# Queries of a cross attention made for two tiles at once, from high and low halves

## The reference

```python
Q = (x @ Wq.T).reshape(B, xN, NUM_HEADS, HEAD_DIM)
KV = (z @ Wkv.T).reshape(B, zN, 2, NUM_HEADS, HEAD_DIM)
K, V = KV[:, :, 0], KV[:, :, 1]
attn = softmax(einsum('bqhd,bkhd->bhqk', Q, K) * SCALE)
O = einsum('bhqk,bkhd->bqhd', attn, V).reshape(B, xN, DIM)
return O @ Wo.T
```

## Time and profile before

| | |
|---|---|
| runs | 1501.46, 1505.46, 1506.04 us; median 1505.46 |
| the profiled execution | 1500.6 us, its span 1498.8 us |
| busy over the span | TensorE matmul 1436.7 us (96%), weight load 1284.1 (86%), VectorE 1087.7 (73%), ScalarE 807.3 (54%), GpSimd 544.1 (36%) |
| DMA | 174.10 MB, 116 GB/s over the span |
| setup block | 3.7 to 19 us |
| cross attention | 19 to 687 us, its first scores at 32.35 us |
| tile 1, tile 13, tile 14, tile 15 begin at | 72.16, 557.03, 597.43, 637.40 us |

### The profile page before, as it was taken

One profiled execution on the slowest core, in us unless ns is written; L12 is line 12 of the kernel. 1 busy time (PEld: TensorE's weight loads), 2 busy tenths in 40 slices (PEclk: granted clock), 3 DMA queues, 4 the chain that ended last, 5 costly groups with the idle time before them and its releaser, 6 DMA issues. The chain is left out here.

```text
span 1498.8 us, 39481 instructions
## 1 busy us (share of the span) xinstructions
PE 1436.7 (96%) x14944; PEld 1284.1 (86%) x14944; DVE 1087.7 (73%) x1941; ACT 807.3 (54%) x1525; POOL 544.1 (36%) x814
## 2 busy tenths in 40 slices
PE   7999999999999999998899998799999999999998
PEld 6888888888888888876788787688999999999997
DVE  3677777777677776775567686797887878787885
ACT  4666666666666666654333434345555555555452
POOL 1222222222222222234866877453332333334232
PEclk9999999999999999999999999799999999999999
DMA  6301101100001100100001104179877878787871
GB/s 238 126 26 30 30 22 28 28 23 27 28 22 28 28 28 22 30 9 1 31 31 38 38 31 156 59 216 317 270 262 256 274 252 268 261 279 244 289 255 46
DMA packets 130733, 174.10 MB, mean 116 GB/s; under 512 B 16953, under 2 KB 89337, under 8 KB 130626
## 3 DMA queue, kind: packets, MB, share of 16 engines
q1 hardware_dynamic: 120242, 145.56, 30.1%
q0 software_dynamic: 10384, 27.05, 5.0%
HBM read 157.18 MB, written 19.06 MB: 118 GB/s over the span
## 5 line engine op out<-in xcount | busy, mean ns | idle before, releaser
L2215 DVE TENSOR_TENSOR split<-raw,split 128x1024 fp32r<-128x1024 f32 x204 | 242.3, 1220 | 6.6 <-ACT split L2155 4.0
L52 PE MATMUL bank<-split_xT,split 128*128 128x256 f32 x768 | 217.1, 283 | 0.4
L54 PE MATMUL bank<-split_xT,split 128*128 128x256 f32 x768 | 216.2, 282 | 0.0
L53 PE MATMUL bank<-split_xT,split 128*128 128x256 f32 x768 | 216.1, 281 | 0.0
L2155 ACT CAST split<-raw 128x1024 fp32r<-128x1024 f32 x202 | 203.2, 1048 | 5.9 <-DMA raw<-in_L_ffn_W_dram 4.0
L596 ACT ACTIVATE Pr<-xa_s,nmax 128x257 f32<-128x257 f32 x256 | 118.7, 473 | 125.1 <-DVE nmax L696 125.1
L2175 ACT ACTIVATE sl<-bank 128x256 f32<-128x256 f32 x115 | 44.2, 384 | 241.8 <-PE bank L54 232.8
L52 PE MATMUL xa_s<-split,split 128*128 128x258 f32 x512 | 150.6, 294 | 1.9 <-DVE split L628 1.9
L52 PEld LDWEIGHTS bank<-split_xT,split 128*128 128x128 f32 x768 | 145.5, 189 | 6.6 <-issue 2.5
L53 PEld LDWEIGHTS bank<-split_xT,split 128*128 128x128 f32 x768 | 145.6, 190 | 3.2
L53 PE MATMUL xa_s<-split,split 128*128 128x258 f32 x512 | 145.8, 285 | 0.0
(11 more groups left out here) (314 smaller groups left out, 3918.5 us busy)
## 6 DMA issues: line engine op xcount, KB each, us to landing
raw<-in_L_ffn_W_dram SPq DMA_DIRECT2D x207, 512.0 KB
raw<-in_ctx_dram SPq DMA_DIRECT2D x64, 256.0 KB, 2.6
out_dram<-x_res SPq DMA_DIRECT2D x16, 256.0 KB
xs<-xn SPq DMA_DIRECT2D x16, 256.0 KB
x_res<-in_x_dram SPq DMA_DIRECT2D x1, 3584.0 KB, 19.0
VL<-v_last_rows SPq DMA_DIRECT2D x128, 2.0 KB, 1.5
raw_o<-in_L_xattn_Wo_dram SPq DMA_DIRECT2D x1, 1024.0 KB, 6.5
raw_q<-in_L_xattn_Wq_dram SPq DMA_DIRECT2D x1, 1024.0 KB, 9.6
```

The source lines that it names most:

```text
L52: pe.matmul(out, lh, rh, start=start, stop=False)
L53: pe.matmul(out, ll, rh, start=False, stop=False)
L54: return pe.matmul(out, lh, rl, start=False, stop=stop)
L2215: vW.done(dve.tensor_tensor(lo, raw, hi.bitcast(F32), ALU.subtract), f"p{c}{q}")
```

## The change

Queries are made in the even tile alone, for the two tiles that come next as a pair: steps 2 and 3 of tile `i` (with `u == 0`) make the first and the second half of Wq for tiles `i + 2` and `i + 3`, with 24 matmuls each, 256 columns wide (two x tiles side by side), three for each product of high and low halves. For that WqT is split in the setup block (four more subtractions), and each turned x tile: `x_out` now copies `bank_o` twice, once to `xnT` (nobody reads it in the new project_q) and once to `xT_hi`, and `x_lo` makes `xT_lo` on VectorE. Each `project_q` half fills all of `bank_o`, and `q_out` copies 512 columns to both `Qp`. x tiles are turned one tile earlier: x tile 1 in the setup block, x tile 2 in step 1 of tile 0, then `i + 3` in step 2 of tile `i`, where `more`; statistics and `normalise` move with them. The second QK tensor goes; it stands in the w13 parts of weight slots 1 and 2, which become one tensor `raw` with slot 0. So wq and wo (2 MB) are loaded at SP's end, behind the last `qk_lo` (`v_QK` at `s_end`), and the other five loads stay in tile 0.

```diff
+        WqT_hi, WqT_lo = sb("WqT_hi", [P, KC, C], F32R), sb("WqT_lo", [P, KC, C], F32R)
+        xT_hi, xT_lo = sb("xT_hi", [P, KC, 2 * P], F32R), sb("xT_lo", [P, KC, 2 * P], F32R)
...
-        def x_out(act, i):
+        def x_out(act, i, slot):
             act.wait_ge(pe_X, i + 1)
-            act.copy(xnT.rearrange("p k q -> p (k q)"), bank_o[:]).then_inc(a_X, 1)
+            act.copy(xnT.rearrange("p k q -> p (k q)"), bank_o[:])
+            act.copy(xT_hi[:, :, slot * P:(slot + 1) * P], bank_o[:].rearrange("p (k q) -> p k q", q=P)).then_inc(a_X, 1)
+        def x_lo(dve, i, slot):
+            at = slice(slot * P, (slot + 1) * P)
+            dve.wait_ge(a_X, i + 1)
+            dve.tensor_tensor(xT_lo[:, :, at], bank_o[:].rearrange("p (k q) -> p k q", q=P), xT_hi[:, :, at].bitcast(F32),
+                              ALU.subtract).then_inc(v_X, 1)
         def rows_of(i):
-            return x_res[:, i % n_tile if isinstance(i, int) else i, :]
+            return x_res[:, i % n_tile, :]
...
                             turn_x(pe, 0)
+                    pe.wait_ge(v_X, 1)
+                    turn_x(pe, 1)
...
                         if n == n_values - 1:
-                            x_out(act, 0)
+                            x_out(act, 0, 0)
+                    x_out(act, 1, 1)
                 @block.vector
                 def _(dve):
                     dve.wait_ge(x_first, 16)
                     statistics(dve, 0)
                     normalise(dve, 0)
-                    for n, (_load, blocks, (hi, lo), width) in enumerate(jobs[:n_split]):
+                    def low(n):
+                        _load, blocks, (hi, lo), width = jobs[n]
                         dve.wait_ge(hi_done, n + 1)
                         dve.tensor_tensor(lo, ring[n % 6][:, 0:len(blocks) * width], hi.bitcast(F32),
                                           ALU.subtract).then_inc(lo_done, 1)
+                    for n in range(n_split):
+                        low(n)
                     dve.tensor_reduce(own_key[:], ident[:].rearrange("p (h t) -> p t h", t=HD), AX_X, ALU.add
...
                     normalise(dve, 1)
-                    dve.wait_ge(lo_done, n_split)
+                    x_lo(dve, 0, 0)
+                    for n in range(n_values, len(jobs)):
+                        low(n)
+                    x_lo(dve, 1, 1)
+                    dve.wait_ge(lo_done, n_split + KC)
+                    dve.wait_ge(v_X, 2)
                     dve.wait_ge(masked, 3 + BT)
         Qp = [spare.w2[:, u, :] for u in range(2)]
         zn_hi, zn_lo = held.parts(held.xT, 0, 2, L)
-        QK = [sb(f"QK{u}", [P, KL, NH, P]) for u in range(2)]
+        QK = [sb("QK0", [P, KL, NH, P]), later_13.rearrange("p k (h t) -> p k h t", t=P)]
         QK_hi, QK_lo = held.parts(held.w13[1], 0, 2, C)
...
             if j % 2 == 0 and (more or u == 0):
-                return 1 - u, j, 2 * (i + 1) + 2, BT * i + NQ + j + 2
+                return 1 - u, j, 2 * i + (6 if u else 4), BT * i + NQ + j + 2
             return None
...
                     if first:
-                        weights.load(sp)
+                        weights.load(sp, False)
                 by_pair(sp, tile)
+                sp.wait_ge(v_QK, s_end)
+                weights.load(sp, True)
...
-                def project_q(i, half, wait_first=True):
-                    pe.wait_ge(a_X, i + 1)
-                    if half == 1 and wait_first:
-                        pe.wait_ge(a_Q, 2 * i + 1)
-                    for m in range(2 * half, 2 * half + 2):
+                def project_q(i, half):
+                    if half == 0:
+                        pe.wait_ge(a_X, i + 2)
+                        pe.wait_ge(v_X, i + 2)
+                    else:
+                        pe.wait_ge(a_Q, 2 * i + 2)
+                    for m in range(2):
+                        w = slice((2 * half + m) * P, (2 * half + m + 1) * P)
                         for k in range(KC):
-                            mm = pe.matmul(bank_o[:, m * P:(m + 1) * P], WqT[:, k, m * P:(m + 1) * P], xnT[:, k, :],
-                                           start=(k == 0), stop=(k == KC - 1))
+                            mm = product(pe, bank_o[:, m * 2 * P:(m + 1) * 2 * P], (WqT_hi[:, k, w], WqT_lo[:, k, w]),
+                                         (xT_hi[:, k, :], xT_lo[:, k, :]), k == 0, k == KC - 1)
                     mm.then_inc(pe_Q, 1)
...
                 project_q(0, 0)
-                project_q(0, 1, False)
                 turn_z(0, 0, 0)
-                pe.wait_ge(a_Q, 2)
-                turn_x(pe, 1)
+                project_q(0, 1)
                 absorb_k(Qp[0], 0)
                 absorb_k(Qp[0], 1)
-                project_q(1, 0)
+                pe.wait_ge(a_Q, 4)
                 pe.wait_ge(a_QK, 2)
                 pe.wait_ge(d_QK, 2)
                 absorb_k(Qp[0], 2)
                 absorb_k(Qp[0], 3)
-                project_q(1, 1, False)
                 for k in range(KL):
...
                         if j == 0 and not first:
-                            pe.wait_ge(a_Q, 2 * min(i + 2, n_tile) if isinstance(i, int) else 2 * i + 4)
+                            if u == 1:
+                                pe.wait_ge(a_Q, min(2 * i + 6, 2 * n_tile) if isinstance(i, int) else 2 * i + 6)
+                            else:
+                                pe.wait_ge(a_X, i + 3)
+                                pe.wait_ge(v_X, i + 3)
                             need(pe, v_OP, i - 1)
...
                             last_values(i - 1)
-                        if j == 2 and not last:
+                        if first and j == 1:
+                            turn_x(pe, 2)
+                        if j == 2 and more:
                             need(pe, v_OP, i)
-                            turn_x(pe, i + 2)
+                            if first:
+                                pe.wait_ge(a_X, 3)
+                                pe.wait_ge(v_X, 3)
+                            turn_x(pe, i + 3)
                         if not (last and j == BT - 1):
...
                             project_o(i - 1)
-                        if j == 2 and more:
-                            project_q(i + 2, 0)
-                        if j == 3 and more:
-                            project_q(i + 2, 1)
+                        if j >= 2 and more and u == 0:
+                            project_q(i + 2, j - 2)
                         if step is not None:
...
-                def q_out(i, slot, halves):
-                    act.wait_ge(pe_Q, 2 * i + max(halves) + 1)
-                    at = slice(halves[0] * C // 2, (halves[-1] + 1) * C // 2)
-                    act.mul(Qp[slot][:, at], bank_o[:, at], SCALE).then_inc(a_Q, len(halves))
+                def q_out(i, half):
+                    act.wait_ge(pe_Q, i + half + 1)
+                    act.mul(spare.w2[:, :, half * C // 2:(half + 1) * C // 2].rearrange("p s (m q) -> p m s q", q=P),
+                            bank_o[:].rearrange("p (m s q) -> p m s q", m=2, s=2), SCALE).then_inc(a_Q, 2)
...
                             qk_hi(s + 1, t, (j + 1) % BT, BT * i + (BT if j < BT - 1 else 2 * BT))
-                        if j == 2 and not last:
-                            x_out(act, i + 2)
+                        if first and j == 1:
+                            x_out(act, 2, 0)
+                        if j == 2 and more:
+                            x_out(act, i + 3, 1 - u)
                         if not (last and j == BT - 1):
...
                         pt_hi(s)
-                        if j >= 2 and more:
-                            q_out(i + 2, u, (j - 2,))
+                        if j >= 2 and more and u == 0:
+                            q_out(i + 2, j - 2)
                 by_pair(act, tile)
...
                             last_rows(i - 1)
-                        if j == 2:
-                            normalise(dve, i + 2)
+                        if first and j == 1:
+                            normalise(dve, 2)
+                        if j == 2 and not last:
+                            normalise(dve, i + 3)
                         dve.wait_ge(a_E, 4 * s + 4)
...
                             z_lo(s + 1)
-                        if j == 1:
-                            if first:
-                                dve.wait_ge(x_rest, 16)
-                            statistics(dve, i + 2)
+                        if first and j == 0:
+                            dve.wait_ge(x_rest, 16)
+                            statistics(dve, 2)
+                        if first and j == 1:
+                            x_lo(dve, 2, 0)
+                        if j == 1 and not last:
+                            statistics(dve, i + 3)
+                        if j == 2 and more:
+                            x_lo(dve, i + 3, 1 - u)
                         if j == 0 and not first:
...
-    def load(self, sp):
-        for dst, src in self.loads:
```

(37 more changed lines are left out.)

## The result

The changed kernel took 1543.08 us (median of 4 runs, 1539.19 to 1545.57), the kernel before 1503.46 beside it: a ratio of 1.0276, with an interval of 1.0257 to 1.0295. It is slower by 2.8%, or 39.6 us. The sign and the places were forecast, the size was not: 1531 with a range up to 1544, and 27.6 us by the sum. The measured median lies in the last microsecond of that range; as a ratio on the median shown before (1505.46), the change comes to 1547, outside it.

The account below looks back on a forecast made before the run. It took TensorE's matmul issue and waits to bound the loop, with a copy chain behind `project_q`. Terms 20.2 - 0.4 + 4.2 + 2.8 + 0.8 = +27.6 us on 1500.6 gave 1528.2, base-adjusted to 1531; range 1514 to 1544.

Parts of the forecast that it names:

- The products: Query matmuls in the even tile: 24 per half take 2.84 us, 5.68 a pair where 7.82 before.
- the wait of 1.5 us: Even tile, step 2: TensorE waits 1.5 us for the low part of x before `project_q`; bounds 1.0 and 1.9.
- step 3 +1.05: Even tile, step 3: 2.84 us of projection replaces 1.79, with no wait to take it up.
- The odd tile becomes tile 14: Odd tiles, without `project_q`, behave like tile 14 of the kernel before: -0.47 us each.
- Rival 3: Loop: two recurring waits make the clock fall in every pair, 7 x 2.8 = 20 us more, 1551; 8%.
- The start: Setup block +3.7 us for six more subtractions, block behind it +0.5, together +4.2; bounds 3 and 5.
- the clock +2.8: Start: TensorE's idle times in the setup cause one more half-speed stretch, +2.8 us; bounds 0 and 5.6.
- Tile 0, +0.8: Tile 0, step 1: turning x tile 2 there adds 0.8 us; bounds 0.4 and 2.0.
- The late weights: wq and wo, loaded behind the last `qk_lo`, land by 675.8; 2.1 us of lateness are hidden, so no cost.
- Rival 1: Loop: TensorE's matmul issue alone decides, so 15 us less, total 1490 or 1492, faster; 6%.
- Rival 2: Even tile, step 2: no wait for `v_X`, so +1.4 us a pair, total 1515 or 1517; 10%.
- Rival 4: Whole kernel: odd tile's gain and even tile's loss cancel, under 4.5 us either way; 4%.

Follow-up runs that it names:

- run 4: Changed kernel with x's low part made before z's and no copy to `xnT` except for tile 0: 1530.31 us.
- run 3: Changed kernel with the odd tile's turn of x in step 3, plus 17 unread matmuls where TensorE waits in the odd tile's step 2: 1533.74 us.
- run 6: Changed kernel with step 2's QK copies shared, ScalarE taking the banks the transposes need first and VectorE the others: 1530.02 us.
- run 2: Changed kernel with the odd tile's turn of x moved from step 2 to step 3: 1541.36 us.
- run 5: Changed kernel with unread matmuls (7 and 10) in TensorE's two idle times of the setup block: 1539.28 us.
- run 1: Kernel before with only the first of four matmuls of each product of `project_q`, waits and copies kept: 1490.46 us, ratio 0.993.
- run 7: Changed kernel with both x tiles turned in the odd tile, z turned behind absorb, step 2's QK copies shared, setup idle times filled: 1509.13 us, ratio 1.005.
- run 8: Kernel before with unread matmuls in TensorE's two waits of tile 0, step 0, and step 2's QK copies shared: 1491.11 us, ratio 0.9922.

## Why the prediction was wrong in size

- *The products, 2.84 us a half; the wait of 1.5 us; step 3 +1.05.* Right: 2.95, 1.53 and +1.08; step 2 of the even tile came to +2.38 (2.3 forecast). Run 4 took 1.08 us off the wait and the tile became 1.08 shorter.
- *The odd tile becomes tile 14, -0.47.* This is the step that failed: +1.04 us. The wait was the one foretold, 2.05 us, and so was its mechanism; but I read from tile 14 that a wait of 2.10 leaves the clock at 1.00, one case with one outcome, and gave "the clock falls in every pair" 8%. It fell in all seven odd tiles and in tile 14. Runs 3 and 6 show that this wait is what it hangs on: filled or shortened, the odd tile takes 39.9 or 39.8 us. Tile 14 came to +1.1 and not -0.4 for the same reason; less the 1.5 of the fall, it is the -0.4. What decides whether a wait of this length costs the clock (runs 2 and 4) stays open. These two terms are 12 us of the 12.4 between the 27.6 forecast and the 40.0 that the traces show at tile 15. Rival 3 had the right event and overpriced it, 1.5 us a fall and not 2.8; of the two waits that it named, the odd tile's is the one that counts.
- *The start +4.2, the clock +2.8.* 7.5 measured, for 7.0: the setup ended 3.76 later (22.86 for 19.10), run 5 puts the clock's part at 2.3, and the remaining 1.4 of the block behind it were put at 0.5.
- *Tile 0, +0.8 on top of an even tile's 3.35.* 3.3 in all, for 4.15. Step 2 cost 2.9 us more and not 2.4, but step 0 took 9.12 us for 9.85, since less of it ran at half speed (granted clock 0.99 there, where it was 0.87).
- *The late weights, nothing.* Right: issued at 705.18 and 705.61 in the changed kernel, landing in 5.7 and 7.9 us, so by 713.5; ScalarE took them at 713.98.
- *The other rivals.* Rival 1 (faster, by issue alone) is refuted by run 1. Rival 2 (no wait for `v_X`) did not come about; run 7 arranges it, and its even tile takes 41.82. Rival 4 is out by the result.
- *An x tile that nobody reads.* A misreading, as run 4 showed. The tile is needed and is turned one tile earlier; the 0.4 us that the sum took off tile 14 stand all the same.
- *A slip.* VectorE's next work waited 3.13 us, not 3.19; nothing hangs on it.
- A half of the projection took 0.123 us a matmul, 2.95 for 24. The isolated gap of the Trainium skill ("TensorE: Matmul & The Clock Gate", Back-to-back issue gap), 109 ns, is 11% under it, so the row was the better guide.
- The clock fell again in every odd tile (0.93 in step 2 of tile 11). The Trainium skill ("TensorE: Matmul & The Clock Gate", HAM oscillation) warns of a loop in which each round's wait costs the clock again, though the waits of its example are longer than the 2.05 us here; I had set it aside on tile 14's evidence.

## What to carry to other kernels

Before matmuls are saved, ask what they cover: here 3.9 us of them a tile covered a chain of about 3.4 (leaving them out gave 0.5), so in this order of the work no cheaper way to make the queries could gain more than 0.5 us a tile, and taking them out of one tile bought waits. A wait of TensorE must be priced twice, by its length and by the half-speed stretch that may follow it, and a single instance without a fall is weak evidence that there will be none. Where TensorE has to wait anyway, matmuls into a free bank cost nothing here and can pay (run 3: 7.6 us). A shorter chain did it too (run 6: 13 us, some 12 of them the clock's).

## What the runs showed of the hardware

- Behind waits of TensorE of 2.05 us the granted clock fell in all seven odd tiles of the changed kernel, in six of seven in run 2 (tile 1, with 2.10, is the exception) and in three of seven in run 4. A fall cost 1.5 us of a tile. Behind 1.41 (run 1), 1.19 (run 6) and 1.53 us (the seven even tiles of the changed kernel) it never did.
- The length of the wait doesn't decide alone: behind 1.97 us the clock fell in run 7 and not in run 5, and behind 2.57 us in run 7 it stayed. What else decides, no run here shows.
- A wait can be hidden in a busy engine's rows: in the kernel before `project_q` took 2.12 us to the next start in step 2 and 1.79 in step 3, for the same 16 records. In run 8, where the copies come earlier, it takes 1.88 in step 2 and the step is 0.28 us shorter, so most of the difference was a wait for the QK copies.
